# A two-layer graph-attention kernel: three ScalarE copies, two VectorE subtractions and the first step's copies and weight load, issued in another order

## The reference

```
layer 0: Q, K, V = x@Wq+bq, x@Wk+bk, x@Wv+bv            (8 heads of 64)
         s = Q K^T / 8 + a[i] + c[j] + b_g + log(adj + 1e-9)   (a, c = x @ w_g halves)
         x1 = softmax(s) V + x
layer 1: q, k = x1@Wq1+bq1, x1@Wk1+bk1;  s = q k^T / sqrt(512), masked where adj == 0
         ctx = (softmax(s), masked) x1 @ Wc
         out = layernorm(x1 + ctx) * gamma + beta
```

## Time and profile before

| | |
|---|---|
| median of 3 runs | 2324.58 us (2323.35 to 2325.12) |
| the profiled execution | 2323.79 us, span 2322.0 us |
| TensorE (PE) busy | 2261.8 us, 97% |
| VectorE (DVE) busy | 1935.1 us, 83% |
| ScalarE (ACT) busy | 1211.2 us, 52% |
| GpSimd (POOL) busy | 979.8 us, 42% |
| mean granted TensorE clock | 0.992 |

### The profile page before, as it was taken

The page is one execution under the profiler, slowest core; times in us unless marked ns, Lnnn a source line. Parts: engine busy times, 40 slices in busy tenths (PEclk is TensorE's granted clock), DMA queues, the critical chain, the costliest instruction groups (busy, mean ns, idle before and its releaser), DMA issues. The chain is left out here.

```text
span 2322.0 us, 39399 instructions
## 1 busy us (share of the span) xinstructions
PE 2261.8 (97%) x13284; PEld 1875.0 (81%) x13284; DVE 1935.1 (83%) x5508; ACT 1211.2 (52%) x3474; POOL 979.8 (42%) x1146
## 2 busy tenths in 40 slices
PE   8999999999999999999999999999999999999986
PEld 6888888888888888888888888888888888888865
DVE  5688888889888888888888888888888898888886
ACT  5445555555555555546555546555555555555542
POOL 0153344453445443444543444543444533444422
PEclk9999999999999999999999999999999999999997
DMA  6333333333333333343333333333433343333321
GB/s 231 115 113 120 109 128 115 128 114 126 116 127 119 128 109 119 114 136 123 125 108 123 114 126 127 119 121 105 132 123 128 112 129 106 127 118 128 105 81 42
DMA packets 187306, 277.98 MB, mean 120 GB/s; under 512 B 24673, under 2 KB 122593, under 8 KB 182881
## 3 DMA queue, kind: packets, MB, share of 16 engines
q1 hardware_dynamic: 186528, 274.42, 35.8%
q10 hardware_dynamic: 576, 1.05, 0.1%
HBM read 166.54 MB, written 108.86 MB: 119 GB/s over the span
## 5 line engine op out<-in xcount | busy, mean ns | idle before, releaser
L1265 POOL TENSOR_TENSOR probs<-probs,rcp 128x512 f32<-128x512 f32 x256 | 290.9, 1152 | 937.2 <-DVE rcp L980 937.0
L742 ACT ACTIVATE probs<-probs,nmax 128x128 f32<-128x128 f32 x1024 | 397.3, 390 | 200.0 <-DVE nmax L970 199.6
L1040 DVE STREAM_TRANSPOSE x1n<-x1T 32x512 f32<-32x512 f32 x512 | 359.5, 702 | 7.6
L1273 POOL TENSOR_TENSOR x_lo<-xT_land,x_hi 128x512 fp32r<-128x512 f32 x124 | 169.2, 1396 | 335.4 <-ACT x_hi L698 335.4
L954 DVE SCALAR_TENSOR_TENSOR bias<-c_rows,a_c,ln_adj 128x128 f32<-128x128 f32 x128 | 136.2, 1122 | 155.9 <-ACT ln_adj L721 144.4
L970 DVE CUSTOM_DVE_ANT_0 probs<-bank,bias 128x128 f32<-128x128 f32 x1024 | 226.9, 285 | 3.2 <-issue 0.4
L223 PE MATMUL bank<-x_hi,wm_hi 128*128 128x512 f32 x512 | 209.5, 409 | 12.9 <-DVE x_lo L1002 12.8
L769 ACT ACTIVATE att<-att,stats 128x128 f32<-128x128 f32 x128 | 50.0, 391 | 326.3 <-DVE stats L1080 326.3
L754 ACT ACTIVATE x1n<-x1n,lnst 128x512 f32<-128x512 f32 x128 | 104.5, 816 | 200.6 <-POOL lnst L1286 200.6
L223 PE MATMUL bank<-x_hi,wk_hi 128*128 128x512 f32 x512 | 204.9, 400 | 2.6 <-DVE x_lo L913 2.5
L223 PE MATMUL bank<-wc_hi,x_hi 128*128 128x512 f32 x512 | 203.6, 398 | 0.0
(11 more groups left out here) (132 smaller groups left out, 5523.5 us busy)
## 6 DMA issues: line engine op xcount, KB each, us to landing
turn_dram<-turned SPq DMA_DIRECT2D x128, 512.0 KB, 2.6
probsT<-turn_dram SPq DMA_DIRECT2D x512, 128.0 KB, 2.7
out<-x1n SPq DMA_DIRECT2D x128, 256.0 KB, 2.0
xn<-in_x SPq DMA_DIRECT2D x126, 256.0 KB, 3.3
xT_land<-in_xT SPq DMA_DIRECT2D x31, 1024.0 KB, 6.8
adj_sb<-in_adj SPq DMA_DIRECT2D x32, 256.0 KB, 3.1
c_rows<-c_dram SPq DMA_DIRECT2D x32, 256.0 KB, 3.2
at_dram<-scratch SPq DMA_DIRECT2D x31, 256.0 KB, 2.0
```

Of the source, the lines that this page charges most:

```text
L742: op = nc.scalar.activation(probs[:, k, :], probs[:, k, :], ACT.Exp, bias=nmax[:, k:k + 1], scale=-1.0, accum_out=sums[:, k:k + 1])
L1040: op = nc.vector.transpose(x1n[b * BLK:(b + 1) * BLK, :, :] .rearrange("p g (c a s) -> p a c g s", c=C, a=P // BLK)[:, a, :, :, :], x1T[a ...
L1265: nc.gpsimd.tensor_tensor(probs[:, half, :], probs[:, half, :], rcp[:, half].unsqueeze(2).to_broadcast([P, HALF, P]), ALU.mult)\
L1273: nc.gpsimd.tensor_tensor(x_lo[:, c, :], xT_land[(t + 1) % 2][:, c, :], x_hi[:, c, :].bitcast(f32), ALU.subtract).then_inc(s["pool_x"], 1)
```

## The change

On ScalarE, k_out(t,2), q_out(t,2) and k_out(t,3) are issued ahead of exp1(u) and q_out(t,3) stays behind it. On VectorE, x1lo(u,2) and x1lo(u,3) are issued ahead of maxima(t,0). In the first step ScalarE copies v 2 and 3 ahead of the first exponentials, and SyncE issues the load of Wc behind spread_c(0). Nothing is added or removed.

```diff
 # SyncE, ahead of its body
             sp.dma_start(bk1_c, bk1).then_inc(s_const1, 16)
-            sp.dma_start(x1T[:, :, :], wc).then_inc(s_wld1["c"], 16)
...
 # SyncE, body, first step
                     spread_c(0)
+                    sp.dma_start(x1T[:, :, :], wc).then_inc(s_wld1["c"], 16)
                     sp.wait_ge(s_lo["q"], C)
                     load_xT(t + 1, 1 - it.par)
...
 # ScalarE, first_step
                 v_out(0, 0)
                 v_out(0, 1)
+                v_out(0, 2)
+                v_out(0, 3)
                 exps(0, 0, 0)
-                v_out(0, 2)
                 exps(0, 0, 1)
-                v_out(0, 3)
                 m_high(0)
...
 # ScalarE, body
                 g_out(u, 3, False)
-                exp1(u)
                 k_out(t, 2)
                 q_out(t, 2)
                 k_out(t, 3)
+                exp1(u)
                 q_out(t, 3)
...
 # VectorE, body
                 residual0(u, 2)
                 residual0(u, 3)
-                maxima(t, 0)
                 x1lo(u, 2)
                 x1lo(u, 3)
+                maxima(t, 0)
                 x1_rows(u, 0)
                 recips(t, 0)
```

## The result

The changed kernel took 2327.13 us in the median of 17 runs (2324.38 to 2331.72), the kernel before 2323.89 us in the median of 17 beside it (2321.48 to 2327.38). The ratio is 1.0016, with a 95% interval of 1.0009 to 1.0024: slower by 3.2 us, 0.16%. The forecast was 2320.2 with a range up to 2326.0, so the sign was missed, and the time lies 1.1 us above the range.

The account below looks back on a forecast made before the run. A ring of engines through the attention's DRAM trip, tied with TensorE, was taken as the bound. -1 us over 29 steps and -3.4 in the first make -4.4 against 2323.79: 2319.4, or 2320.2 as a median; range 2309 to 2326.

Parts of the forecast that it names:

- The ring: Logarithm, minima, exp1, attention's DRAM trip, low part, layer norm, next logarithm: about 70.0 to 70.1 us per step beside TensorE.
- Part one: ScalarE's three copies ahead of exp1: TensorE's k wait moves to the context product; -0.05 us per step on the ring.
- the 70.05: Repeated step: the ring's time in us before the change's terms, with an average DMA wait of 1.53 in it.
- Part two: VectorE's low parts ahead of the maxima: waiting for ScalarE's high parts adds 0.2 us per step, bounds 0 and 0.64.
- Part three: First step: gate column's trip no longer queued behind Wc, so the bias starts sooner; -3.4 us, ends 0 and -6.
- the forecast's -1 for the 29 steps: Repeated steps: 70.05 + 0.2 - 0.05 = 70.2 us against the mean 70.23, so -1 us over 29.
- A: Repeated steps: the forecast itself, the ring holds; 2314 to 2325 us, chance 0.64.
- B: Repeated steps: TensorE is the bound, so each loses its removed waits, 0.8 to 1.1 us; 2293 us, chance 0.05.
- C: GpSimd's earlier x_lo runs into VectorE's attention1 (line 1087), some 0.7 us per step on the ring; 2340 us, chance 0.08.
- D: First step gives nothing, as c_rows shares the queue with Wc right behind it; 2323.5 us, chance 0.11.

Follow-up runs that it names:

- TensorE's 0.68 us pad: The changed kernel with three unused matmuls ahead of the first y product in each repeated step: 2329.95 us, 2.8 us above the changed kernel.
- k_alone: The kernel before with only the three k and q copies moved ahead of exp1: 2325.05 us, ratio 1.0008.
- xlo_alone: The kernel before with only x1's last two low parts moved ahead of the maxima: 2331.46 us, ratio 1.0031.
- first_alone: The kernel before with only the first step's edits, v copies first and Wc's load behind the gate column's trip: 2321.68 us, ratio 0.9993.
- short_ring_after: The changed kernel with ScalarE's exponentials of a half pair and a y copy ahead of the copy awaiting the attention's trip: 2295.30 us, 0.9882 against the kernel before.

## Why the prediction was wrong

**What bounds the kernel: right.** The ring through the attention's trip holds the changed kernel, the wait moves from the k copy to the context product, and TensorE's 0.68 us pad vanishes. The ring alone was put at 70.0 to 70.1, and the table bears that out: the terms of the kernel before make 70.21, and its last term is 23.39 where the undisturbed boundaries take 23.24, since the y parts wait for TensorE in some of them, which leaves 70.06. What the sum had no term for is that such waiting stays in the changed kernel too: 23.31 in place of 23.24, 0.07 per step or 2 us, over half of it in the one step in which the clock fell (24.36).

**Part one, "Step part one: -0.05 on the ring": this is the step that failed.** The copies cost the ring nothing where the forecast looked, exp1 waits for the minima as before. But the trip through DRAM was taken to be as long with the change as without it, its average wait of 1.53 us being part of the 70.05. The write half grew by 0.34, the read half fell by 0.15, the low part's term by 0.04: +0.15 per step in place of -0.05, 29 x 0.20 = 6 us. k_alone has the longer write half too (2.52), xlo_alone and first_alone have not (2.35 and 2.29), so it belongs to this part: code packets meet the write more often once TensorE no longer stands at pv.

**Part two, "an estimate of 0.13 at the first and 0.06 at the second, 0.2 us per step":** 0.24 in the table, the mechanism right and the term small by 1 us in all. xlo_alone measured the part at +7.5 us, all of it on the ring, and the M product's wait, which it removed, was worth nothing.

**Part three, "First step: -3.4":** 3.19 in the profiled execution, 2.3 in the medians of first_alone. The column's trip lost 3.0 of its 6.3 us.

Together: 2 + 6 + 1 = 9 us, which is what lies between the forecast's -1 for the 29 steps and the measured +8.0. The first step gave 0.2 less than forecast, and the end of the run, for which there was no term, is 0.7 shorter: -4.4 + 9 + 0.2 - 0.7 = +4.1, as in the profiled execution.

**The rivals.** A was right as a mechanism, and its range ended too low, since it let the DMA vary in the ring's favour and not against it. B has its answer in short_ring_after: TensorE's own step is 69.13, so 2295 was to be had, once the trip is off the ring. C: x_lo starts 2.82 after exp1, 0.13 us after the last operation of line 1087 begins (2.69), and the four still take 1.14, in all 32 groups. The rule that stood against it (the Trainium skill, GPSIMD Engine Reference, Specifications: GpSimd contends with vector instructions that have two SBUF inputs) has no cost here for an operation that began first; one of line 1087 that begins second wasn't tried. Where the low parts of line 1002 run beside GpSimd for long, both engines are slower (3.15 and 1.62 above against 1.28 and 1.29), as that rule has it. D was wrong, the column is no longer behind Wc.

## What to carry to other kernels

Look for the ring before the gap: where a wait of the busiest engine is removed and another engine's chain closes over the same step, the wait only moves, and edits that each look good can together be worth nothing until the one link that holds the ring, here a DMA wait with ready work behind it, is taken out. Order the edits by that: moving one half pair's exponentials and one y copy ahead of the waiting copy turned this change from +3 into -23 us. And a DMA trip on a ring is no constant: price it by its distribution over the steps, and ask which other traffic it will meet when an engine runs earlier.

## What the runs showed that was not expected

- A 256 KB write to DRAM takes 2.03 us from its issue to the next issue when no code packet is near, and up to 4.3 us when one 16 KB packet of TensorE's code starts in its first 1.6 us. 105 such packets come in a run, and which steps they hit repeats from kernel to kernel: of the eight long writes of the kernel before, four of its variants have at least seven in the same steps.
- With TensorE as the bound, three matmuls of 0.227 us per step cost 26.2 us over the run, 5 more than their own time; the waits for turned probabilities are longer by 5.5 us beside them, and why they are wasn't tried.
- 84 small matmuls in the warm-up took 17.9 us and 34 took 4.15, 0.21 each against 0.12. The projections behind the 84 follow one another by 0.43 us until 26.8 us into the run and by 0.23 from there on; behind the 34 that change comes at 11.3 us.
- A long write can cost TensorE more than its length: in one step of the changed kernel the granted clock fell to half right behind the wait, and that step took 73.71 us.
